# Graph layer on one core: the sums of an iteration share one PSUM bank, one-hots come two iterations ahead, and eight groups of gathered rows are held instead of four

## The reference

```python
src = node_feature[edge_src]
parts = [relu(node_feature)]
for t in range(3):
    msg = relu(src @ W_e[t].T + b_e[t])
    msg = where((edge_type == t)[:, None], msg, 0)
    parts.append(segment_sum(msg, edge_dst, num_segments=N))
agg = concatenate(parts, axis=1)
for t in range(3):
    o = agg @ W_n[t].T + b_n[t]
    updated = where((node_type == t)[:, None], o, updated)
x = layernorm(x + updated + node_feature)
```

## Time and profile before

| what | us |
|---|---|
| median of 3 runs (lowest, highest) | 1012.33 (1012.32, 1013.22) |
| the profiled execution | 1012.83 |
| its span, first to last instruction | 1010.9 |
| POOL busy | 756.2 |
| PE busy | 700.0 |
| DVE busy | 512.2 |
| ACT busy | 132.3 |

### The profile page before, as it was taken

How to read it: one execution, slowest core, us unless ns; L and a number is a source line. 1 busy time by engine, 2 the same in 40 slices (tenths; PEclk the granted TensorE clock), 3 DMA queues, 4 the chain that set the end, 5 groups by cost and what they waited for, 6 DMA issues and landing times.

```text
span 1010.9 us, 9119 instructions
## 1 busy us (share of the span) xinstructions
PE 700.0 (69%) x2671; PEld 459.3 (45%) x2671; DVE 512.2 (51%) x1187; ACT 132.3 (13%) x350; POOL 756.2 (75%) x808
## 2 busy tenths in 40 slices
PE   6761477776767767776767687667876676768576
PEld 4430354454444544544444455444544454445344
DVE  6999544454445444544544454445444542443433
ACT  3581001000100100010001001000100010121010
POOL 7777777777777777777777777777777777777774
PEclk9895557777876877677778767786677776797869
DMA  7774323222222222222222222212223232222221
GB/s 222 237 272 90 55 54 82 53 78 81 53 78 79 53 80 60 71 78 55 79 79 52 80 67 64 78 53 81 78 53 91 80 91 78 61 69 79 62 66 40
DMA packets 52653, 83.75 MB, mean 83 GB/s; under 512 B 15059, under 2 KB 34688, under 8 KB 52606
## 3 DMA queue, kind: packets, MB, share of 16 engines
q0 software_dynamic: 25312, 51.89, 19.9%
q1 hardware_dynamic: 24734, 27.41, 8.5%
q10 hardware_dynamic: 2560, 3.88, 1.3%
HBM read 70.32 MB, written 12.80 MB: 82 GB/s over the span
## 4 chain that ended last, share of the span: by engine, by line
POOL 65%; issue 22%; DVE 5%; DMA 4%; PE 2%; SPq 0%; ACT 0%; POOLq 0%; DVEq 0%
POOL tab L510 63%; DMA tab<-message_table,idx_t 3%; POOL xg L506 2%; PE ps L1219 2%; DVE tab L870 2%; DMA dst_raw<-in_dst 1%; DVE src_raw L760 1%; DVE dst_raw L758 0%; DVE first_f L736 0%; DVE h L1000 0%; PE ps L1260 0%; SPq L335 0%; ACT acc L585 0%; POOLq L122 0%; DVE loop_f L732 0%
## 5 line engine op out<-in xcount | busy, mean ns | idle before, releaser
L510 POOL DMA_INDIRECT tab<-message_table,idx_t x720 | 680.1, 945 | 219.4 <-issue 216.1
L1219 PE MATMUL ps<-work,tab 128*128 128x126 f32 x1440 | 272.1, 349 | 273.7 <-DMA tab<-message_table,idx_t 273.4
L1219 PEld LDWEIGHTS ps<-work,tab 128*128 128x128 f32 x1440 | 241.4, 252 | 370.4 <-issue 361.8
L923 DVE TENSOR_TENSOR work<-key_t,ps 128x504 f32<-128x504 f32 x180 | 122.0, 679 | 419.0 <-PE ps L1219 417.0
L1260 PE MATMUL ps<-wn_t,stage 128*128 128x384 f32 x294 | 150.2, 637 | 1.4 <-DVE stage L1027 1.4
L506 POOL DMA_INDIRECT xg<-in_x,esrc_t x68 | 71.0, 1043 | 21.6 <-issue 18.9
L1260 PEld LDWEIGHTS ps<-wn_t,stage 128*128 128x128 f32 x294 | 69.0, 265 | 29.6 <-issue 23.0
L931 DVE TENSOR_TENSOR acc<-ps,acc 128x126 f32 x216 | 61.3, 284 | 24.4 <-PE ps L1219 13.2
L1252 PE MATMUL ps<-wn_t,stage 128*128 128x384 f32 x98 | 73.2, 846 | 0.0
L1251 PE MATMUL ps<-bn_row,ones 1*128 1x384 f32 x98 | 69.5, 803 | 1.2 <-DVE mv L1005 0.9
L626 ACT ACTIVATE xst<-ps 128x256 f32<-128x256 f32 (+1 forms) x36 | 13.7, 381 | 416.2 <-PE ps L1193 416.2
(11 more groups left out here) (167 smaller groups left out, 486.8 us busy)
## 6 DMA issues: line engine op xcount, KB each, us to landing
tab<-message_table,idx_t POOLq DMA_INDIRECT x720, 2.5
message_table<-tab SPq DMA_DIRECT2D x24, 384.0 KB, 3.4
wn_raw<-message_table SPq DMA_DIRECT2D x22, 384.0 KB, 3.4
xg<-in_x SPq DMA_DIRECT2D x11, 256.0 KB, 4.0
work<-in_x ACTq DMA_DIRECT2D x10, 256.0 KB, 4.1
out<-xg SPq DMA_DIRECT2D x10, 256.0 KB, 3.4
xg<-in_x,esrc_t POOLq DMA_INDIRECT x68
wn_raw<-in_L_gnn_W_n ACTq DMA_DIRECT2D x1, 768.0 KB, 9.9
```

The source lines that it names most:

```text
L510: pool.indirect_dma_start(msg[:, slot, :], None, table, bass.IndirectOffsetOnAxis(ap=rows, axis=0)).then_inc(signal, 16)
L923: dve.tensor_tensor(hot[:, n * g:n * g + n, :], keys.broadcast_to((P, n, T * WIN)), iota_ps.rearrange("p (o c) -> p o c", o=1).broadcast_t ...
L1219: ins = pe.matmul(sums_bank(nth), msg[:, GC * g + c, :], hot[:, GC * g + c, :], start=(c == 0), stop=(c == GC - 1))
```

## The change

- **Bank of the sums.** The four groups of iteration j write four strips of 126 columns of one bank, `SUM_PS[j % 2]`, and not three banks in turn. DVE adds all four to `acc` behind the fourth sum. In iteration 44 the four sums have four different places and are added one by one.
- **One-hots.** There are two sets of them (`hots`), one in `work`, the other where edge orders and indices lay in setup (`first_src`); DVE makes those of iteration j+2 in iteration j. Those of iterations 0 and 1 are made in setup.
- **Slots.** 32 slots (RING = 8 groups): 24 in `tab`, 8 in `order_f`, which held the edge orders. POOL waits for the sum of eight groups before.
- **Stages.** In iteration j DVE does `finish_acc` of tile j-1 and `finish_h` of tile j-2 behind the adds, and `finish_y` of tile j-3 at its start. PE does the whole linear layer of tile j-2 (bias, x and types) behind group 1 of iteration j, and both the turn and `place_selfs` of tile j-1 behind group 2. They share a bank, so ACT's `finish_x` now waits for `self_placed`; before, `place_selfs` waited for `finish_x`. In iteration 44 the linear layer's first part of tile 43 stands behind group 2, its type parts ahead of group 3, as before.
- **Early work.** PE's sums and turns of early edges share bank 2 and one semaphore, `e_placed`, and its messages are made an iteration later.

```diff
-AGG = (0, 1, 2)
+SUM_PS = (0, 1)
...
                 for g in range(NG):
-                    if j > 0:
-                        pool.wait_ge(group_summed, NG * (j - 1) + g + 1)
-                    for slot in range(GC * g, GC * g + GC):
-                        gather(slot, idx_t[:, 2 * j + slot // HC, slot % HC:slot % HC + 1], gathered[g])
+                    n = NG * j + g
+                    if n == OWN:
+                        pool.wait_ge(hot_ready, 1)
+                    if n >= RING:
+                        pool.wait_ge(group_summed, n - RING + 1)
+                    for c in range(GC * g, GC * g + GC):
+                        gather(n % RING * GC + c % GC, idx_t[:, 2 * j + c // HC, c % HC:c % HC + 1],
+                               gathered[n % RING])
...
                 act.wait_ge(fin_xt[z], nth + 1)
+                if z == 0 and placed:
+                    act.wait_ge(self_placed[0], nth + 1)
...
+                if last:
+                    finish_sd(j - 2)
                 if fin:
-                    mask_selfs(j - 1)
-                    finish_x(j - 1, first=isinstance(j, int) and j == 1)
-                if j > 1:
-                    finish_sd(j - 2)
+                    finish_x(j - 1, first=j == 1)
...
+                    if j + 2 < NI:
+                        one_hot(j + 2, g)
+                    if g == 0 and j > 2:
+                        finish_y(j - 3, j - 3)
...
+                    if last:
+                        if g == FIN + 1:
+                            dve.wait_ge(stage_acc[0], j)
+                        add_group(g)
+                        if g == 1:
+                            finish_h(j - 2, j - 2)
+                        if g == FIN:
+                            finish_acc(j - 1, j - 1, 0, sums_ahead(j, g) + 1)
+                            finish_y(j - 2, j - 2)
...
+                for g in range(NG):
+                    add_group(g)
+                if j > 0:
+                    finish_acc(j - 1, j - 1, 0, sums_ahead(j, NG))
+                if j > 1:
+                    finish_h(j - 2, j - 2)
...
-                    if j > 1 and g == 0:
-                        linear_types(j - 2, 0, 1, 2)
-                    if j > 1 and g == 1:
-                        linear_types(j - 2, 0, 3, T)
...
                     if g == 1:
-                        if early:
-                            early_make(j, 0)
+                        if j > 1:
+                            finish_linear(j - 2, first=j == 2)
...
                     if g == FIN:
-                        if early:
-                            early_make(j, 1)
-                        if fin:
-                            finish_turn(j - 1, j - 1, loads, first=start)
+                        if j > 0:
+                            finish_turn(j - 1, j - 1, loads, first=j == 1)
+                            place_selfs(j - 1, j - 1)
...
-                    if g == FIN + 1 and fin:
-                        place_selfs(j - 1, j - 1)
-                        linear_open(j - 1, first=start)
+                        if last:
+                            linear_open(j - 1)
```

More of the change, by code:

```diff
@@ L45 @@
 NG, GC = 4, 4
+RING, OWN = 8, 6
 CT = NG * GC
@@ L56 @@
 FIN = 2
-BEHIND = 2
 WIN = 42
@@ L144, in build @@
         work = sb("work", [P, max(CT * T * WIN, 4 * XB * D)])
-        hot = work[:, 0:CT * T * WIN].rearrange("p (c k) -> p c k", k=T * WIN)
+        hots = [whole.rearrange("p (c k) -> p c k", k=T * WIN)
+                for whole in (work[:, 0:CT * T * WIN], first_src[:, 0:CT * T * WIN].bitcast(F32))]
         gen_hots, gen_iota = work[:, 0:GW], work[:, 2 * XB * D:2 * XB * D + GW]
@@ L249, in build @@
         hot_ready = sem("hot_ready")
-        gathered = [sem(f"gathered{g}") for g in range(NG)]
+        gathered = [sem(f"gathered{g}") for g in range(RING)]
         group_summed, added = sem("group_summed"), sem("added")
@@ L396, in iteration @@
                     if j == tile + 1:
-                        sp.wait_ge(e_turned, (tile + tiles + 1) // 2)
+                        sp.wait_ge(e_placed, (tile + tiles + 1) // 2)
                         load_fin(tile, tiles)
@@ L1029, in finish_acc, with iteration, add_group @@
                                   ).then_inc(stage_acc[z], 1)
-            def iteration(j, fin=True, extra=None, more=True):
-                bases_of = load_bases(j, 0 < j <= NE)
-                if j > 1:
-                    finish_acc(j - 2, j - 2, 0, sums_ahead(j))
+            def iteration(j, extra=None):
+                last = j == NI - 1
+                bases_of = load_bases(j, 1 < j <= NE + 1)
+                def add_group(g):
+                    add_sums(sums_ahead(j, g), sums_at(j, g), bases_of[g])
@@ L1046, in iteration @@
-                    if g == 1 and 0 < j <= NE:
-                        early_add(j - 1, bases_of[NG])
-                    if g == 1 and j < NE:
-                        early_hot(j)
-                    if g == (FIN if more else 1) and j > 1:
-                        finish_h(j - 2, j - 2)
-                    if g == FIN + 1 and j > 1:
-                        finish_y(j - 2, j - 2)
-                    if g == FIN + 1 and j < NE:
-                        early_select(j)
-                    if g == 1 and extra is not None:
-                        finish_acc(ORDER[extra], extra, 1, sums_ahead(j, g) + 1)
@@ L1058, in iteration @@
-                    if g == FIN and not more:
-                        finish_acc(j - 1, j - 1, 0, sums_ahead(j, g) + 1)
-                if not more:
-                    finish_acc(ORDER[KE], KE, 1, ALL_SUMS)
+                    if j + 2 < NI:
[4 more added lines that the diff above has]
+                        if j > 1:
+                            dve.wait_ge(stage_acc[0], j - 1)
+                        if 1 < j <= NE + 1:
+                            early_add(j - 2, bases_of[NG])
+                        if extra is not None:
+                            finish_acc(ORDER[extra], extra, 1, sums_ahead(j))
@@ L1071, in _ @@
             dve.wait_ge(setup_copied, len(UNITS))
-            for g in range(NG):
-                one_hot(0, g)
+            for j in range(2):
+                for g in range(NG):
+                    one_hot(j, g)
             first_rows()
@@ L1252, in linear_open, with linear_types @@
                 pe.matmul(lin, stage[z][:, 0, :], wn_t[:, 0, :], start=False, stop=False)
[L1254 removed]
+            def linear_types(nth, z):
                 lin = ps[:, LIN_PS[z], 0:T * D]
[L1257 to L1259 removed]
+                pe.wait_ge(stage_acc[z], nth + 1)
+                for i in range(1, T + 1):
                     ins = pe.matmul(lin, stage[z][:, i, :], wn_t[:, i, :], start=False, stop=(i == T))
[L1261 to L1262 removed]
+                ins.then_inc(fin_lin[z], 1)
             def finish_linear(nth, z=0, first=False):
```

231 lines of the change are left out of this document (121 added, 110 removed).

## The result

| | before | after |
|---|---|---|
| median of 6 runs each (lowest, highest), us | 1012.87 (1012.32, 1013.22) | 1017.32 (1014.35, 1019.26) |
| ratio, 95% interval | | 1.0039 [1.0029, 1.005] |
| the profiled execution / its span, us | 1012.83 / 1010.9 | 1018.11 / 1016.2 |

The change costs 0.39%. In the runs shown ahead of the prediction the median before was 1012.33; with three more it is 1012.87. The 1017.32 lies 2.7 us above the forecast of 1014.6 and 0.1 us above the range for 8 in 10. Taken as a ratio, 1.0039 on 1012.33 is 1016.3: inside that range, and 0.5 above 1015.8, the upper edge of the forecast's own range. The six runs of the changed kernel spread over 4.9 us, those of the kernel before over 0.9 us.

A forecast was written before the change was run, and what follows sets the result against it. POOL issuing gathers back to back was taken as the bound; 0 in setup and 45 iterations plus 2.3 us at the end (0.8 chain, 1.5 clock) on 1012.33 gave 1014.6, own range 1014.3 to 1015.8, 8 in 10 1012.4 to 1017.2.

The forecast's parts named there:

- Slots, 0 us: POOL waiting for a sum eight groups back, not four, takes no wait away: 0 us, gain at most 3.3.
- the 11 pieces by PE: Idle pieces before 11 gathers with PE as releaser, 3.3 us in all, taken as issue cost of 0.30 us each.
- One-hots, bank, stages, 0 us up to iteration 43: Extra setup one-hots, later adds and stages an iteration apart stay hidden by POOL's gathers: 0 us.
- a first gather that is not at 99.8: Sign of a wrong prediction in the profile: POOL's first gather starting at another time than 99.8 us.
- The chain of the end at full clock, +0.8: Iteration 44, tile 42's linear layer to the last sum with PE at 2.4 GHz: last sum at 1001.42, +0.8 us.
- The clock, +1.5: PE at 1.2 GHz for part of iteration 44's chain adds 1.5 us to the 0.8, making +2.3.
- F: Moment in us when PE's clock rises to full in iteration 44; taken as 992, between 990 and 993.
- the 995.36 of full clock: Forecast end in us of tile 42's linear layer in iteration 44 if PE runs at 2.4 GHz.
- Rival 3: PE's clock low to the end of the chain, F = 996 or later: +4.3 to +5, 1016.6 to 1017.3; chance 0.1.
- F = 996: Latest clock rise taken as upper bound for the end of iteration 44: +4.3 us.
- The last sum was to start 1 to 4 us behind 1000.6: Profile sign of being right: PE's last sum starts 1 to 4 us after 1000.6, behind tile 43's type parts.
- `finish_y`, gain 0, at most 0.45: Tile 42's `finish_y` leaving DVE's end, between last add and `finish_acc`: gain 0 us, at most 0.45.

The follow-up runs named there:

- b_ring8: The kernel before with the 32 slots alone, against the kernel before on chip 4: 1162.12 to 1172.54 us, ratio 1.0087.
- a_ring4: The changed kernel with 16 slots instead of 32, against the kernel before on chip 12: 1160.36 to 1165.8 us, ratio 1.0043.
- a_best4: The changed kernel with 16 slots and its last iterations' work reordered, against the kernel before on chip 0: 1172.12 to 1169.86 us, ratio 0.9987.

## Why the prediction came out as it did

**Slots, 0 us.** Right on the first chip, and by its reason: the 11 pieces by PE were issue. What the prediction had not seen is that this need not hold where the sums do not keep up with POOL. On chip 4 the same edit costs 10 us (b_ring8), although there POOL does wait for sums, the one case in which it had seemed able to gain.

**One-hots, bank, stages, 0 us up to iteration 43.** Right: 720 gathers without a stall. The first one was 0.6 us later, before the loop, and the last 0.7; that term was not in the sum, and the prediction itself had named a first gather that is not at 99.8 as a sign of being wrong. What in setup takes the 0.6 us is open.

**The chain of the end at full clock, +0.8.** The picks to the end of the root take 1000.51 to 1002.57, 2.06 as forecast; `linear_open` to the last sum 1002.79 to 1006.31, 3.52 as forecast. The order of the chain is the one that was laid out.

**The clock, +1.5.** This is the term that was mis-sized. The formula was 988.5 + 6.65 + (F - 988.5) / 2 for the end of tile 42's layer. With F = 999.1 it gives 1000.45, and the trace has 1000.40. That it fits to 0.05 is luck, since the work began at 989.02 and not at 988.5, which makes 1000.71; but the form was right and F was wrong. 992 was taken from the rise at 990 before, as a moment of the program and not by what PE had done ahead of it: before, PE had worked at 1.2 GHz without a gap since 980.75.

And PE's work ahead of it was foreseen wrongly. The prediction had PE idle for most of 977 to 985.7, since iteration 43 would have less for PE behind group 1. It has more: tile 41's whole linear layer stands there now. PE is busy all of 976 to 981, the clock comes up at 978.6, PE runs out of work at 982.6, and the clock falls at 985.4, just ahead of group 0 of iteration 44. From there PE enters with an idle time of 3.81 us and another wait of 0.37 us behind it, and is busy at half rate from 989.02 to 999.1. Tile 42's layer ends 5.0 us behind the 995.36 of full clock, where 1.5 was forecast; some 0.6 of it is that the rows of group 1 land later, 4.4 is the clock.

Rival 3, clock low to the end of the chain, is what the trace shows; it had 0.1, and its 1016.6 to 1017.3 reaches the measured median; the F = 996 that was called the upper bound was too low. The last sum was to start 1 to 4 us behind 1000.6, and it started 5.7 behind. So the chain was foreseen and its price was not: that the measured ratio lies inside the range is owed to the range's width, which took in this rival.

The Trainium skill, "TensorE: Matmul & The Clock Gate", section "What's actually happening", has the throttled state as the default, released by activity. The trace agrees in direction: the clock fell at 985.4, behind idle time (PE was busy for 1.29 us of 981 to 986), and was at 0.50 behind it. It rose again only 10.1 us after PE's last wait.

**`finish_y`, gain 0, at most 0.45.** From the last add to `finish_acc` it is now 1007.50 to 1007.82, 0.32, and was 0.65. So the piece did cost 0.33, within the bound of 0.45. `finish_acc` now starts 0.03 us behind the end of the add, so the wait behind the add of 996.97 had another cause than the add's completion. Small, but the reason given was wrong.

**The sum.** The last sum starts 5.7 us later (1006.31 against 1000.62): 0.8 for the chain, 5.0 for the late end of tile 42's layer, less some 0.15 of the handovers, which were forecast a little too long. Behind the start of the last sum the span is 0.4 us shorter, most of it `finish_y`. That makes 5.3, by which the spans differ. The profiled execution is 0.8 us above the changed kernel's median. The spread of its six runs roughly goes with their mean clock: 1014.35 us at 0.758, 1015.43 at 0.753, 1016.65 at 0.749, and the three longest, 1017.99, 1018.11 and 1019.26, at 0.745, 0.750 and 0.746. That fits a chain whose length hangs on when the clock rises; it is argued from six pairs and was not isolated.

**What is shown and what is not.** That the whole loss on the first chip lies in the chain of the last iteration is read from its trace. That undoing one step of it would win the time back was not tried there, since all experiments ran where PE's signals come late; nor was theory B, the waits around the shared banks, tried apart, though the trace shows no such wait in the chain of the end. What the experiments do show is that the whole change with 16 slots costs 0.43% (a_ring4), that it costs nothing that can be told with its end laid out otherwise (a_best4, on another chip), that tile 42's layer alone does not cost it, and that 32 slots have a cost of their own where PE's signals come late. Open stay why these signals are late and what makes PE fall back in the first iterations with 32 slots.

## What to carry to other kernels

Lay out the last iteration by what has to run between the last landings and the end, and price each PE step there at both rates of its clock: a matmul that waits there comes out of an idle time, and here the half rate added 4.4 us to a chain that at full clock would have cost 0.8. When the clock will rise is not to be read off as a time of the old kernel: the change also moves the work that stands ahead of it. A deeper ring in front of an engine that never waits buys nothing, and where the consumer is the slower one it lets the producer run ahead without ending sooner; check the ring alone, under other conditions too. Compare variants only with the old kernel on the same chip: here the same kernel differed by 15% between two sets of runs, and a term of 0 on the one (the slots) was 10 us on the other.

## What was not expected of the hardware

- The same kernel took 1013 us on the first chip and 1160 to 1172 us on three others, with the same time for a gather's issue (0.94 us) and for its rows to arrive (2.1 to 2.2 us). What was late there were PE's signals: the one for a turn came 1.2 to 9.8 us behind the end that the profile gives it, as medians of the twelve runs, against 0.01.
- PE was busy without a gap from 989.02 and still had half its clock until 999.1; the matmuls of that stretch are bias, x and type parts, a placing of self edges and one group's sums. Before, the clock rose at 989.9, PE having been busy since 980.75.
- Putting 16 more slots to use, with no work added to the loop, cost 0.87% on chip 4, where PE's signals come late, and nothing on the first chip by its trace.
